# Gated attention state in 32-row chunks on column and row tiles, and the last down products split in halves

## What is computed

```python
# layer 0 feed-forward
h = silu(gate) * up
y = einsum('bsi,hi->bsh', h, w_down)
# layer 1 attention: q, k have 32 features, v is x itself (512 features)
q = softmax(x @ Wq.T); k = sigmoid(x @ Wk.T); v = x; gf = log_sigmoid(-k)
def step(S, inp):                       # over chunks of tokens, S is [32, 512]
    A = tril(einsum('bid,bjd,bijd->bij', qh, kh, exp(Bi - Bj)))
    o = A @ vh + (qh * exp(Bh)) @ S
    S = S * exp(Blast) + (kh * exp(Blast - Bh)).T @ vh
go = o @ Wog.T + x @ Wig.T
o = o * rsqrt(mean(o*o) + eps) * g_norm_w * silu(go)
return o @ Wo.T
```

## Time and profile before

| | us |
|---|---|
| median of 3 runs (919.4 to 919.83) | 919.53 |
| profiled execution | 918.98 |
| its span, first to last instruction | 917.1 |
| PE busy | 895.9 (98%) |
| DVE busy | 641.8 (70%) |
| ACT busy | 427.2 (47%) |
| POOL busy | 309.6 (34%) |

### The profile page before, as it was taken

The page is one execution under the profiler, slowest core; times in us unless marked ns, Lnnn a source line. Parts: engine busy times, 40 slices in busy tenths (PEclk is TensorE's granted clock), DMA queues, the critical chain, the costliest instruction groups (busy, mean ns, idle before and its releaser), DMA issues.

```text
span 917.1 us, 13278 instructions
## 1 busy us (share of the span) xinstructions
PE 895.9 (98%) x4688; PEld 709.7 (77%) x4688; DVE 641.8 (70%) x1215; ACT 427.2 (47%) x725; POOL 309.6 (34%) x288
## 2 busy tenths in 40 slices
PE   9999999999999999999999999999999999999994
PEld 7777877876888888888778776777867878888883
DVE  6755754587987798798679758877789786544413
ACT  5544333544444533634573676454653463332222
POOL 3001300015776444444333332231226232734342
PEclk9999999999999999999999999999999999999998
DMA  8532021203100000000000300010201543232411
GB/s 285 184 109 93 17 87 36 81 13 104 46 24 1 1 0 1 1 1 1 27 20 1 104 1 1 2 46 1 93 1 24 183 156 110 66 119 69 141 66 46
DMA packets 43973, 54.18 MB, mean 59 GB/s; under 512 B 6113, under 2 KB 25858, under 8 KB 43906
## 3 DMA queue, kind: packets, MB, share of 16 engines
q1 hardware_dynamic: 42082, 49.11, 16.5%
q0 software_dynamic: 1824, 4.22, 1.4%
HBM read 42.78 MB, written 10.52 MB: 58 GB/s over the span
## 4 chain that ended last, share of the span: by engine, by line
PE 63%; DVE 8%; issue 3%; ACT 2%; POOL 1%; DVEq 0%; ACTq 0%; POOLq 0%
PE ps L41 14%; PE ps L43 14%; PE ps L42 14%; PE ps L2415 7%; PE ps L2416 7%; DVE acc L1787 4%; PE ps L2520 1%; PE ps L2506 1%; PE ps L2447 1%; PE ps L2532 1%; PE ps L2513 1%; DVE junk L1990 0%; PE ps L2657 0%; PE ps L2603 0%; DVE state L1891 0%
## 5 line engine op out<-in xcount | busy, mean ns | idle before, releaser
L1787 DVE SCALAR_TENSOR_TENSOR acc<-ps,gu_scale,acc 128x512 f32<-128x512 f32 x264 | 197.5, 749 | 48.2 <-ACT acc L1448 28.4
L2415 PE MATMUL ps<-xt_hi,gu_val 128*128 128x512 f32 x352 | 140.6, 400 | 3.2 <-PEq L71 1.5
L2416 PE MATMUL ps<-xt_lo,gu_val 128*128 128x512 f32 x352 | 137.3, 390 | 0.0
L1448 ACT ACTIVATE acc<-ps,gu_scale 128x512 f32<-128x512 f32 x88 | 60.6, 689 | 89.0 <-PE ps L2416 88.9
L2320 POOL TENSOR_TENSOR fsg<-fsg,acc 128x512 f32<-128x512 f32 x44 | 59.2, 1345 | 108.8 <-DVE acc L1787 104.8
L2415 PEld LDWEIGHTS ps<-xt_hi,gu_val 128*128 128x128 f32 x352 | 66.0, 188 | 28.7 <-DVE acc L1787 11.5
L2416 PEld LDWEIGHTS ps<-xt_lo,gu_val 128*128 128x128 f32 x352 | 66.1, 188 | 12.1
L2325 POOL TENSOR_TENSOR fh_lo<-fsg,fh_hi 128x512 fp32r<-128x512 f32 x44 | 58.9, 1338 | 42.8 <-ACT fh_hi L1460 42.8
L41 PE MATMUL ps<-dn_hi,fh_hi 128*128 128x512 f32 x176 | 69.2, 393 | 1.1 <-POOL fh_lo L2325 1.1
L42 PE MATMUL ps<-dn_hi,fh_lo 128*128 128x512 f32 x176 | 68.7, 390 | 0.0
L43 PE MATMUL ps<-dn_lo,fh_hi 128*128 128x512 f32 x176 | 68.6, 390 | 0.0
(11 more groups left out here) (317 smaller groups left out, 2165.8 us busy)
## 6 DMA issues: line engine op xcount, KB each, us to landing
mw_raw<-in_w SPq DMA_DIRECT2D x16, 512.0 KB, 3.6
a_nib<-in_gate_up_packed SPq DMA_DIRECT2D x88, 64.0 KB, 2.5
x<-x SPq DMA_DIRECT2D x16, 256.0 KB, 3.6
mw_raw<-x SPq DMA_DIRECT2D x8, 512.0 KB, 4.3
out<-mw_raw SPq DMA_DIRECT2D x8, 512.0 KB, 3.0
xt_raw<-in_xT SPq DMA_DIRECT2D x3, 1024.0 KB, 4.9
x<-in_x SPq DMA_DIRECT2D x3, 1024.0 KB, 5.5
a_nib<-in_down_packed SPq DMA_DIRECT2D x8, 256.0 KB, 3.2
```

The lines of the kernel that those rows point to most:

```text
L1448: act.activation(acc[part][u // 2 % 2][:, :], ps[:, FG, :], ACT.Copy, scale=gu_scale[:, part * IT + j, 0:1]).then_inc(s_g0, 1)
L1787: dve.scalar_tensor_tensor(out=a[:, :], in0=ps[:, FG + c, :], scalar=gu_scale[:, part * IT + j, c:c + 1], in1=a[:, :], op0=ALU.mult, op1=A ...
L2415: pe.matmul(ps[:, FG + c, :], gu_val[:, o, c, :], xt_hi[b % 2][:, c, :], start=True, stop=False)
L2416: pe.matmul(ps[:, FG + c, :], gu_val[:, o, c, :], xt_lo[b % 2][:, c, :], start=False, stop=True).then_inc(s_gu, 1)
```

## The change

- The state is kept once, as [4 chunks of 32 rows, 128 columns] (chunk j of 128 features on rows 32j to 32j+31), no longer as four copies of [32, 512]. `update` is four float32 products with 32 weight columns, one on each column group of the array, into columns 0 to 127 of bank AS = 6.
- `outputs` is four float32 products scores by x of 128 columns, then four products queries by state with 32 weight rows each, one on each row group, into four banks (0 to 3). In block 0 only banks 3 and 4 are free: the chunks go in two pairs, each with its scores products and then its state products.
- `q_low`, `state_high` and `state_low` are gone; `next_state` works on 128 columns and not 512; `k_end` has one copy and not four. DVE runs `mask` ahead of `next_state`.
- `update` and `scores` stand directly behind `transpose_features`; for n = 1 and 2 `transpose_x` moves behind them. It now writes bank 5, so it waits for that tile's pairs and queries to be taken, and the next tile's features wait for its copy.
- In tile (1,0) the first 6 of 12 matmuls of `project_out(0,0)` run ahead of `update`, the other 6 behind `transpose_x`.
- `transpose_qk` uses bank 3 and waits for `take_o` of the block's last tile; `project_out` of blocks 0 to 2 has one bank in place of two, and waits for the residual of the tile before; `gate_x` moves between banks with waits to match.
- The last hidden tile's down products: the 8 matmuls that need only the high part first, then a wait for the low part, then 4.

```diff
-        k_end = put("k_end", [P, TB, REP, DK], 74)
+        k_end = put("k_end", [P, TB, DK], 74)
-        state = [put(f"state{i}", [P, C], 104 + 2 * i) for i in range(2)]
-        s_parts = [put(f"s_parts{i}", [P, C], 148 + 2 * i, F32R) for i in range(2)]
+        state = [put(f"state{i}", [P, P], 104 + i / 2) for i in range(2)]
...
-        G, Y, F, A, O, S, OT = 0, 2, 3, 4, 5, 6, 7
+        TOK, Y, F, AS, BC, OT = 3, 4, 5, 6, 6, 7
...
+        def out_at(n, j):
+            return (3 + j % 2, slice((j // 2) * P, (j // 2 + 1) * P)) if n == 0 else (j, slice(0, P))
...
             def next_state(n, t):
                 i = TB * n + t
                 dve.wait_ge(s_su, i + 1)
-                if i >= 2:
-                    dve.wait_ge(s_sl, i - 1)
+                dve.wait_ge(s_a, i + 1)
+                dve.wait_ge(s_o, i)
...
+            def last_hidden_tile(k):
+                j = k % IT
+                pe.wait_ge(s_hh, k + 1)
+                for t in range(TB):
+                    hi = f_hi[k % HS][:, t * P:(t + 1) * P]
+                    pe.matmul(ps[:, FY + t, :], hi, dn_hi[:, j, :], start=False, stop=False)
+                    pe.matmul(ps[:, FY + t, :], hi, dn_lo[:, j, :], start=False, stop=False)
+                pe.wait_ge(s_hl, k + 1)
+                for t in range(TB):
+                    ins = pe.matmul(ps[:, FY + t, :], f_lo[k % HS][:, t * P:(t + 1) * P], dn_hi[:, j, :], start=False, stop=True)
+                ins.then_inc(s_dn, 1)
...
             def transpose_x(k, c):
...
-                    if c:
-                        pe.wait_ge(s_xtl, KC * (k - 1) + c)
-                    else:
-                        pe.wait_ge(s_sg, KC * (k - NBLK - 1) - 1)
+                    i = TB * (k - NBLK - 1) + c
+                    pe.wait_ge(s_pt, i + 1)
+                    pe.wait_ge(s_qt, i + 1)
...
             def transpose_qk(n):
                 pe.wait_ge(s_qkf, n + 1)
-                pe.wait_ge(s_at, TB * n)
+                pe.wait_ge(s_ot, TB * n)
...
             def update(n, t):
...
-                pe.matmul(ps[:, S, :], k_end[:, t, :, :].rearrange("p r d -> p (r d)"), x[n][:, t, :], start=True, stop=True).then_inc(s_su, 1)
+                for j in range(KC):
+                    ins = pe.matmul(ps[j * DK:(j + 1) * DK, AS, 0:P], k_end[:, t, :], x[n][:, t, j * P:(j + 1) * P],
+                                    start=True, stop=True, skip_group_check=True)
+                ins.then_inc(s_su, 1)
...
             def outputs(n, t):
...
-                ins = pe.matmul(ps[:, O, :], at[t % 2][:, :], x[n][:, t, :], start=True, stop=first)
-                if not first:
-                    pe.wait_ge(s_ql, i + 1)
-                    pe.wait_ge(s_sl, i)
-                    ins = pe.matmul(ps[:, O, :], q_parts[t % 2][:, :], s_parts[1 - t % 2][:, :], start=False, stop=True)
+                for chunks_of_o in ((0, 1), (2, 3)) if n == 0 else (range(KC),):
+                    for j in chunks_of_o:
+                        bank, cols = out_at(n, j)
+                        ins = pe.matmul(ps[:, bank, cols], at[t % 2][:, :], x[n][:, t, j * P:(j + 1) * P], start=True, stop=first)
+                    if not first:
+                        if n == 0 and 2 in chunks_of_o:
+                            pe.wait_ge(s_two, t)
+                        for j in chunks_of_o:
+                            bank, cols = out_at(n, j)
+                            d = slice(j * DK, (j + 1) * DK)
+                            ins = pe.matmul(ps[:, bank, cols], q_rows[t % 2][d, :], state[1 - t % 2][d, :], start=False, stop=True)
+                        if n == 0 and 0 in chunks_of_o:
+                            ins.then_inc(s_two, 1)
                 ins.then_inc(s_o, 1)
...
-            down_tiles(IT * NBLK - 1, range(TB))
+            last_hidden_tile(IT * NBLK - 1)
             for n in range(NBLK):
                 for t in range(TB):
                     transpose_features(n, t)
+                    early = 2 if n == 1 and t == 0 else 0
+                    if early:
+                        out_bank_left(0, 0)
+                        pe.wait_ge(s_sg, 3)
+                        project_chunks(0, 0, range(early))
+                    update(n, t)
+                    scores(n, t)
                     if 0 < n < LAST:
                         transpose_x(NBLK + n + 1, t)
-                    update(n, t)
-                    scores(n, t)
-                    if n:
+                    if early:
+                        project_chunks(0, 0, range(early, KC))
+                    elif n:
                         project_out(n - 1, t)
```

More of the change, by code:

```diff
@@ L1189, in feed_forward_to_end @@
         s_s = sem("state_ready")
-        s_sh = sem("state_hi_done")
-        s_sl = sem("state_lo_done")
+        s_two = sem("two_chunks_done")
         s_o = sem("o_done")
@@ L1303, in token_bank @@
         def token_bank(n):
-            return A if n else FG + 1
+            return TOK if n else FG + 1
         def tokens(n):
@@ L1506, in take_queries @@
                     act.wait_ge(s_o, i - 1)
[L1507 to L1514, removed]
+                act.activation(q_rows[t % 2][:, :], ps[:, feature_bank(n, t), 2 * P:3 * P], ACT.Copy).then_inc(s_qt, 1)
             def take_o(n, t):
@@ L1521, in take_o @@
                 act.wait_ge(s_pl, KC * n)
-                act.activation(o_tok[:, :], ps[:, O, :], ACT.Copy).then_inc(s_ot, 1)
+                if n == 0:
+                    chunks_out, chunks_in = "p (h a c) -> p a h c", ps[:, 3:5, 0:2 * P].rearrange("p a (h c) -> p a h c", c=P)
+                    act.activation(o_tok[:, :].rearrange(chunks_out, a=2, c=P), chunks_in, ACT.Copy).then_inc(s_ot, 1)
+                else:
+                    act.activation(o_tok[:, :].rearrange("p (j c) -> p j c", c=P), ps[:, 0:4, 0:P], ACT.Copy).then_inc(s_ot, 1)
             def square_o(n, t):
@@ L1862, in features @@
                 key_copies(n)
[L1864 to L1868, removed]
-                    part = slice(a * DK, (a + 1) * DK)
-                    ins = dve.tensor_tensor(q[part, :], ps[part, feature_bank(n, t), 2 * P:3 * P], q[part, :].bitcast(F32), ALU.subtract)
-                ins.then_inc(s_ql, 1)
             def mask(n, t):
@@ L1891, in next_state @@
                     dve.scalar_tensor_tensor(out=state[t % 2][:, :], in0=state[1 - t % 2][:, :], scalar=dec[:, t:t + 1],
-                                             in1=ps[:, S, :], op0=ALU.mult, op1=ALU.add).then_inc(s_s, 1)
-            def state_low(n, t):
-                i = TB * n + t
-                dve.wait_ge(s_sh, i + 1)
-                low = slice(P // 2, P)
-                dve.tensor_tensor(s_parts[t % 2][low, :], state[t % 2][low, :], s_parts[t % 2][low, :].bitcast(F32),
-                                  ALU.subtract).then_inc(s_sl, 1)
+                                             in1=ps[:, AS, 0:P], op0=ALU.mult, op1=ALU.add).then_inc(s_s, 1)
             def o_low(n, t):
@@ L2117, in _ @@
                 for t in range(TB):
-                    q_low(n, t)
+                    mask(n, t)
                     next_state(n, t)
-                    mask(n, t)
                     if 0 < n < LAST:
                         x_low(NBLK + n + 1, t)
-                    state_low(n, t)
                     if n == 0 and t == 0:
@@ L2583, in out_bank_left @@
                     pe.wait_ge(s_wl, 4)
-                pe.wait_ge(s_r, max(i - 1, TB * n))
-                if t == 0:
-                    pe.wait_ge(s_ot, TB * n + TB)
+                pe.wait_ge(s_r, max(i - 1, TB * n) if n == LAST else i)
+                if t == 0 and n < LAST:
+                    pe.wait_ge(s_sg, KC * n + 3)
+                elif t == 0:
+                    pe.wait_ge(s_ot, TB * NBLK)
             def project_out(n, t):
```

53 lines of the change are left out of this document (29 added, 24 removed).

## The result

The changed kernel takes 920.82 us (median of 20 runs, 920.53 to 922.39), beside 919.47 us (20 runs) of the kernel before: 1.35 us more, ratio 1.0015, 95% interval 1.0009 to 1.0022. The sum had +2.0. The profiled execution is 920.81 us, its span 919.0 us against 917.1 before; the granted clock is 0.996 in both. DVE fell from 70% to 66%, and PE still works 97% of the span.

What follows compares the result with a forecast made beforehand. PE, busy 98% of the span, was taken as the bound. Terms 8.0 - 4.2 - 1.4 - 1.1 + 0.75 + 0.7 - 0.7 = +2.0 us gave 921.6 us by the median, range 918.6 to 924.2 (0.83).

Steps and rivals of the forecast that it cites:

- outputs, 11 tiles: Tiles of blocks 1 to 3 with a state: outputs grow from 1.10 to 1.53 us, +0.43 each, +4.7.
- scores, ten tiles: First feature transpose to scores falls from 1.28 to 0.93 us, bound by the pair: 0.35 saved in each of ten tiles.
- start of block 2: In tile (2,0) transpose_x waits for q_rows, which ACT takes only after silu, gated and p_high: +0.7 us.
- start of block 1: Tile (1,0): six early projections hide the silu, but transpose_x waits for q_rows: -0.7 us, 2.1 without that wait.
- What tiles cost: Each short tiled group pays a drain at both sides: eight products cost 0.55 us on columns, 0.63 on rows.
- The load of 0.11 behind a row group: On PE, the weight load behind each row group is hidden by nothing: 0.11 us of the group's 0.63.
- Waits that go: PE's waits for the low part of the last hidden tile, -1.4 us, and for masked scores and a projection, -1.1.
- Waits that come: New PE waits: transpose_qk(1) for o_tok +0.75 us, start of block 2 +0.7, start of block 1 net -0.7.
- A: Rival: the 0.20 drain and 0.11 load behind 17 row groups are not paid, 5.3 us less: 916.3, faster; chance 0.10.
- Its half, the load hidden: Rival: only the load behind the 17 row groups is hidden, 1.9 us less: 919.7, same; chance 0.13.
- B: Rival: halves of a float32 product run one after another on a tile, adding rounds of 0.11 us: 927.6; chance 0.07.
- C: Rival: bank 5, shared by features and transposed x, costs 0.4 us in six tiles of blocks 1 and 2: 924.0; chance 0.10.

Runs made afterwards that it cites:

- e1: The kernel before with one part of the change alone, the last hidden tile's down products in halves: 917.94 us, ratio 0.9984.
- e2: The changed kernel with ACT taking the queries of a block's first tile ahead of the last p_high: 920.09 us, ratio 1.0011.
- e8: The changed kernel with queries taken ahead of the pairs and, in nine tiles, queries by state moved between update and scores: 918.72 us, ratio 0.9988.
- e9: The changed kernel with the 128-column transpose of q_state ahead of the two 64-column ones in transpose_features: 920.64 us, one run.
- e11: The kernel of e2 with ACT taking the next tile's pair ahead of this tile's o_tok: 919.55 us, ratio 1.0001.
- e6: The changed kernel with the four column-tile products of update issued twice in every tile: 920.95 us, ratio 1.0014.
- e10: The kernel of e2 with no products of project_out(0,0) ahead of update in tile (1,0): 920.27 us, ratio 1.0011.
- e3: The changed kernel with the first six products of gate_x(0,3) put ahead of transpose_qk(1): 920.83 us, ratio 1.0014.
- e7: The changed kernel with all twelve products of project_out(0,0) behind the transposes of x in tile (1,0): 923.86 us (4 runs), ratio 1.0039.
- e4: The changed kernel without the products of queries by state in all 14 tiles that have them: 912.12 us, one run.

## Why the prediction was right, and which of its steps were off

The range held, and so did the forecast's own of 919.9 to 923.3: 920.82 is 0.8 under 921.6. Of its three outcomes the prediction had given slower 0.50 and same 0.40, and the same came: a loss of 0.15%, whose interval excludes zero, within the 0.2% that it had named as its bound. Its forecast stood 0.2 us beyond that bound, the result 0.5 us short of it.

| term | predicted | measured, and where |
|---|---|---|
| outputs, 11 tiles | +0.43 each | +0.31 (1.41 less 1.10) in eight; +0.42 in the three that a projection follows |
| outputs, 3 tiles of block 0 | +1.06 each | +0.92 (2.02 less 1.10) |
| scores, ten tiles | -0.35 each | -0.23 (1.05 less 1.28) |
| halves | -1.4 | -1.43; e1 alone -1.6 |
| masked scores, projection | -1.1 | -1.2 by starts: 0.6 in (3,3), 0.3 in (3,2), 0.3 in (0,3) |
| `transpose_qk(1)` | +0.75 | wait of 0.79 |
| start of block 2 | +0.7 | +0.69; e2 gives 0.89 back |
| start of block 1 | -0.7 | -0.5 (6.1 and not 6.6 from gate_o to outputs, of it 0.3 the wait for k_end) |

With -0.2 in each of the four other tiles and +0.1 for the tiles without a state part, the measured parts are 3.7 + 2.8 + 0.1 - 2.3 - 0.7 - 1.4 - 1.2 + 0.8 + 0.7 - 0.5 = +2.0, where PE moved by 1.92 between the two traces. That the medians are 1.35 apart and not 1.9 is outside this account.

- **What tiles cost** was the main step, and its price was right but for one term. The distances of 0.09 ahead and 0.20 behind, read from two rows of another stage, came again: the row group of eight takes 0.43 to the next start in blocks 1 to 3 and 0.42 in block 0. The Trainium skill, page "TensorEngine Tiling (Array Packing)", section Key Properties, has the mode change drain the engine; the trace agrees, with 0.20 us from a group's last start to the next instruction where a round takes 0.11, and e8 has the same 0.21 from 32 rows of weights to 64.
- **The load of 0.11 behind a row group** was the mis-sized term of outputs. The prediction read it where a 512-column product follows the group and charged it where feature transposes follow. Behind a projection or scores products it is there again (0.34 between starts for 0.23 in the last tile of blocks 1 to 3, 0.71 for 0.61 in block 0); behind the first transpose only 0.03 shows, 0.06 for 128 weight columns (e9), and that falls where scores wait for the pair. So outputs are cheaper by 8 x 0.12 + 3 x 0.14 = 1.4 us in all.
- **Scores** were over-valued by nearly the same amount, 10 x 0.12 = 1.2. The prediction took the end of the transposes as what binds the pair. It is ACT's o_tok, which starts 0.14 behind the first transpose and lasts 0.49 to the pair's start; the two were taken to start together. With o_tok out of the way (e11) the transposes bind, at 0.99. That update itself is free, the prediction's other claim, is shown by e6. These two errors have one root: without the load the transposes start 0.11 earlier, and o_tok does not. They offset each other in the tiles of blocks 1 and 2, whose periods grew by 0.02 to 0.10 where +0.08 was predicted. That was luck, since the prediction saw neither.
- **Waits that go.** The halves were right, and e1 shows them alone. The masked scores and the projection gave what was expected, and half of it lay beside the waits in brackets. Nothing came in their place.
- **Waits that come.** All three came at their predicted places, with 0.79, 0.85 and 1.36. The prediction's value for (1,0) held because it was worked out through gated(0,3) and p_low (q_rows at 4.0 behind gate_o; measured 563.44 + 0.26 - 559.64 = 4.06). Its aside, that 2.1 would be had without the wait for q_rows, was wrong: e2 and e10 show p_low late by the same 1.2. The price of `transpose_qk(1)` was right. e3 did not take it away: with the transposes six products later the exponentials on ACT hold o_high(0,3), and 0.6 of the 0.8 comes back as a wait for o_low.
- **Rivals.** A is out: 0.20 is seen behind every row group, and e8 shows it again. Its half, the load hidden, is what the trace has in the 11 of the 17 groups that transposes follow, but did not decide because scores lost nearly as much. The prediction had A decide from 1.2 us, 0.07 a group; by its own numbers (921.6, bound at 921.4) 0.2 us, 0.01 a group, were enough. B is out: L2534 x8 is 0.50 long, two rounds of four. C is out: `transpose_x` in the six full tiles has no wait.

From (0,3) to (1,0) the parts close as well: 0.92 - 0.25 + 0.79 - 0.32, less 0.26 for the projection's wait, is 0.88, and the period grew by 0.96.

What stays open: why the medians are 0.5 us nearer than the traces, why only one of e7's four executions shows the low mean clock, and what `transpose_qk(1)` would be worth on another order of ACT.

## What to carry to other kernels

A short tiled group costs more than twice its arithmetic: eight products took 0.52 us for two rounds of 0.11 (e4), about 0.1 ahead of the group, 0.1 inside it and 0.1 behind it; so tile what runs in long groups, or put the short group where another engine's work is waited for anyway, as update is here. Ahead of pricing the removal of a wait, ask what the same data's next consumer waits for: of the waits taken away here, the halves' and the one in (2,0) came out in full, the pair's by half, and three others (silu, q_rows in (1,0), `transpose_qk`) by 0.2 us at most. Moving work on one engine also moves what stands behind it in another engine's program, as the exponentials did in e3. And when a change bundles parts, run the smallest one alone: here the one-line reordering of the last down products gains 1.6 us, and the rest of the change, which is most of its lines, costs 2.9.

## What the runs showed of the hardware

- In one traced execution (e7) PE stood 1.32 and 1.35 us, 0.8 us of work apart, and the granted clock fell to 0.50 (1.2 GHz) in the second of them and stayed there for some 7 us; three more executions of that kernel have the usual mean clock. With single idle times of 1.36 (changed kernel), 1.20 (e2) and 1.32 (e10) it stayed at 1.00.
- How much of a weight load is seen behind a row group depends on what follows: 0.03 us for a transpose with 64 weight columns, 0.06 with 128 (e9), 0.10 for scores products in block 0 and 0.11 for a projection's 512-column product (changed kernel), as behind the column groups.
- Sixteen products on column tiles add 0.21 us to eight, so two more rounds of four are 0.11 each (e6). The last of eight products starts 0.15 after the first on column tiles and 0.23 on row tiles.
